# Layers two and three of a GraphSAGE kernel: 28 of 196 edge blocks as dense products of edge counts

## The reference

```
def _sage_layer(x, src, dst, inv_deg, W_self, W_neigh, b):
    agg = segment_sum(x[src], dst, num_segments=N_NODES)
    return x @ W_self + (agg * inv_deg[:, None]) @ W_neigh + b

h = relu(layernorm(x))
h = relu(_sage_layer(h, ..., W0_self, W0_neigh, b0))
h = relu(_sage_layer(h, ..., W1_self, W1_neigh, b1))
x = x + _sage_layer(h, ..., W2_self, W2_neigh, b2)
# second block: attention over the same edges (8 heads, edge scores s[src] + s[dst],
# softmax over the edges of each dst), output projection, batch norm, feed-forward, batch norm
x = x + L1_gnn(relu(layernorm(x)), ...)
```

## Time and profile before

| what | us |
|---|---|
| median of 3 runs | 6346.12 (6343.15 to 6388.92) |
| span of the profiled execution | 4316.7 |
| what lies between that span and the median | 2029.4 |
| layer one, first tile to first tile of layer two | 39.5 to 1036.3 |
| layer two | 1036.3 to 2025.4 |
| layer three, first tile to last tile | 2025.4 to 2985.6 |
| attention and feed-forward, to the end | about 1310 |

### The profile page before, as it was taken

How to read it: one execution, slowest core, us unless ns; L and a number is a source line. 1 busy time by engine, 2 the same in 40 slices (tenths; PEclk the granted TensorE clock), 3 DMA queues, 4 the chain that set the end, 5 groups by cost and what they waited for, 6 DMA issues and landing times. The chain is left out here.

```text
span 4316.7 us, 79500 instructions
## 1 busy us (share of the span) xinstructions
PE 3538.7 (82%) x15834; PEld 2475.2 (57%) x15925; DVE 2153.1 (50%) x6078; ACT 488.3 (11%) x1111; POOL 3031.3 (70%) x3154
## 2 busy tenths in 40 slices
PE   4898888888988888888888888888777777776798
PEld 3566565565655555655566665655655555555544
DVE  6434333333333333333455554555577777777733
ACT  4000000000000000000011101101011111111122
POOL 5777777777777777777777777776777777777200
PEclk9999999999999999999999999999788988897999
DMA  6444434434344344344444444445655555554411
GB/s 203 127 129 124 125 105 125 124 106 143 105 123 124 104 124 123 105 123 127 130 140 136 139 139 136 142 136 153 163 146 157 148 156 148 159 147 137 126 60 60
DMA packets 284796, 563.69 MB, mean 131 GB/s; under 512 B 104638, under 2 KB 176133, under 8 KB 279691
## 3 DMA queue, kind: packets, MB, share of 16 engines
q0 software_dynamic: 150528, 414.45, 33.7%
q10 hardware_dynamic: 70180, 89.46, 6.2%
q1 hardware_dynamic: 63974, 58.59, 4.4%
HBM read 487.19 MB, written 73.45 MB: 130 GB/s over the span
## 5 line engine op out<-in xcount | busy, mean ns | idle before, releaser
L763 POOL DMA_INDIRECT arena<-h_table,idx_v x2292 | 2183.6, 953 | 725.7 <-issue 692.9
L897 PE MATMUL banks<-arena 128*128 x5856 | 1465.2, 394 | 353.1 <-SPq L790 248.2
L897 PEld LDWEIGHTS banks<-arena 128*128 128x128 f32 x5856 | 1107.3, 194 | 678.2 <-issue 494.5
L842 DVE TENSOR_SCALAR arena<-iota_t,dst_e 128x128 f32<-128x128 f32 x2928 | 849.8, 306 | 797.2 <-PE banks L897 515.9
L1282 POOL DMA_INDIRECT arena<-vs_table,idx_v x764 | 766.6, 1003 | 232.8 <-issue 229.1
L900 PE MATMUL banks<-zeros 128*128 128x512 bf16 x2108 | 584.4, 385 | 4.6 <-issue 0.7
L1500 PE MATMUL banks<-arena 128*128 x1952 | 519.8, 417 | 53.1 <-DVE arena L1844 53.1
L1500 PEld LDWEIGHTS banks<-arena 128*128 128x128 f32 x1952 | 367.1, 199 | 193.1 <-issue 119.9
L952 DVE TENSOR_SCALAR small<-banks 128x1 f32<-128x1 f32 x147 | 23.3, 158 | 674.9 <-PE banks L901 674.9
L900 PEld LDWEIGHTS banks<-zeros 128*128 128x128 bf16 x2196 | 218.8, 100 | 202.2 <-issue 12.8
L1020 ACT ACTIVATE lhs<-banks 128x512 f32<-128x512 f32 x147 | 87.8, 597 | 2135.3 <-PE banks L911 2135.1
(11 more groups left out here) (265 smaller groups left out, 2505.3 us busy)
## 6 DMA issues: line engine op xcount, KB each, us to landing
arena<-h_table,idx_v POOLq DMA_INDIRECT x2292
arena<-dst_dram SPq DMA_DIRECT2D x14, 1792.0 KB
arena<-vs_table,idx_v POOLq DMA_INDIRECT x764
h_table<-arena ACTq DMA_DIRECT2D x11, 1024.0 KB, 7.5
h_early<-arena ACTq DMA_DIRECT2D x10, 1024.0 KB
vs_table<-arena ACTq DMA_DIRECT2D x49, 132.0 KB
x_dram<-arena ACTq DMA_DIRECT2D x49, 128.0 KB
hln_dram<-arena ACTq DMA_DIRECT2D x49, 128.0 KB
```

What stands on the lines that cost most here:

```text
L763: pool.indirect_dma_start(ring[:, s * BJ + j, 0:width], None, table, bass.IndirectOffsetOnAxis(idx_v[:, half, n * BJ + j:n * BJ + j + 1], ...
L842: dve.tensor_scalar(onehot[:, j, :], iota_t[:], dst_e[:, bass.ds(b * BJ + j, 1)], None, ALU.is_equal).then_inc(W["onehot_made"], 1)
L897: pe.matmul(agg[:, 0:D + 1], onehot[:, j, :], ring[:, (b % SLOTS) * BJ + j, 0:D + 1], start=False, stop=False).then_inc(W["onehot_used"], 1)
```

## The change

Of each seven blocks one may be picked whose `dst` values span at most COUNT_W = 41 nodes; 28 blocks are picked (NC), 168 stay in the list that is gathered (NB2). For a picked block the sum over its edges is written as a product: a matrix of counts (source node by `dst` offset, 6272 x 41) times the node rows.

1. **Picking.** In layer one, ahead of tile 5, `pick_tables_vector` and `pick_tables_tensor` choose the blocks and make new lists and spans: 62 VectorE instructions, each waiting for the one before, and six rounds with TensorE. `batch_tables_vector` moves from ahead of tile 8 to ahead of tile 3, `late_ends_vector` from ahead of tile 16 to ahead of tile 7. `batch_tables_scalar` (four DMAs) moves from behind layer one to behind tile 7 in layer one, and ScalarE waits there until they are done.
2. **Counting.** In tiles 8 to 23 of layer one, seven count blocks in every four tiles: VectorE makes two one-hots for each of the four columns (`low_hot`, 128 wide, and `count_hot`, 2016 wide, bf16), TensorE multiplies them into four banks (16 products of 128x512 bf16), ScalarE converts 2009 columns to int16, and each seventh time stores 3.6 MB to `counts_dram`.
3. **Folding.** For each of the 49 source tiles of the layer that is being made, ScalarE loads 128 x 1148 counts, converts them to fp32, and TensorE multiplies them with the tile's rows in `h_nodes`: CSLOTS = 9 fp32 products of 128x128 by 256, accumulated over all tiles in five banks. In layer one this is done in tiles 25 to 48, two in each; in layer two one in each tile. `folded_rows_vector` copies the 1148 sums into NV = 3 extra slots of the ring.
4. **The next layer** (`sums2`, `onehots2`) goes for each tile through its blocks of the list and then through its virtual blocks, with two sets of span and offset (`span_of`). Pairs of a layer: 168 + 48 and 3 + 48, 267 in all.
5. The products of zeros stay only in tiles 0 to 7 of layer one (four for each pair) and in layer three (one for each pair). The degree is kept from layer one (`inv_deg`), so `means` is one instruction in the layers behind it. In layer three `between` comes behind the blocks of the list.

The core of the diff:

```diff
+COUNT_W = 41
+TABLES_AT, PICK_AT, LATE_AT, COUNT_FROM = 3, 5, 7, 8
+COUNT_GROUP = 7
...
+        def count_block_vector(dve, i):
+            for j in range(BJ):
+                at = bass.ds(i * BJ + j, 1)
+                dve.wait_ge(counted, i * BJ + (COUNTED + j - 1))
+                dve.tensor_scalar(low_hot[j % 2], count_iota[:, 0:P], count_low[:, at], None, ALU.is_equal).then_inc(coded, 1)
+                dve.tensor_scalar(count_hot[j % 2], count_iota, count_code[:, at], None, ALU.is_equal).then_inc(coded, 1)
+
+        def count_block_tensor(pe, i):
+            pe.wait_ge(counts_taken, i + TAKEN)
+            for j in range(BJ):
+                pe.wait_ge(coded, i * (2 * BJ) + (CODED + 2 * j + 2))
+                for n in range(0, HOT_W, BE):
+                    to = min(n + BE, HOT_W)
+                    last = pe.matmul(banks[:, 4 + n // BE, 0:to - n], low_hot[j % 2], count_hot[j % 2][:, n:to], start=j == 0, stop=j == BJ - 1)
+                last.then_inc(counted, 1)
...
+        def counts_scalar(act, l, m, half, more=True):
+            s = m * 2 + half
+            act.wait_ge(counts_in[half], m * 16 + (COUNTS_IN[half] + 16 + 16 * l * ((NT + 1) // 2 - half)))
+            act.wait_ge(counts_used, s + (COUNTS_USED + l * NT - 1))
+            apart(act)
+            act.activation(counts[half], counts16[half], ACT.Copy).then_inc(counts_ready, 1)
+            if more:
+                act.wait_ge(counts_ready, s + (READY + l * NT + 1))
+                counts_load(act, s + 2, half)
...
+        def fold_tensor(pe, l, m, half):
+            s = m * 2 + half
+            pe.wait_ge(W["h_made"], since("h_made", l, s + 1))
+            pe.wait_ge(counts_ready, s + (READY + l * NT + 1))
+            apart(pe)
+            for c in range(CSLOTS):
+                n = min(P, CCOLS - c * P)
+                last = pe.matmul(banks[0:n, 3 + c // 2, c % 2 * D:c % 2 * D + D], counts[half][:, c * P:c * P + n], h_nodes[:, s, :],
+                                 start=False, stop=False)
+            last.then_inc(counts_used, 1)
...
+            def sums2(t):
+                wait(pe, W["mean_made"], since("mean_made", l, t))
+                pe.matmul(agg[:, 0:D], zeros[:, 0:P], zeros[:, 0:D], start=True, stop=False)
+                for h in range(2):
+                    b0, b1, off = span_of(pe, t, h)
+                    with pe.Fori(b0, b1 + 1) as b:
+                        pe.wait_ge(W["rows_ready"], since("rows_ready", l, b % NB2 + 1))
+                        slot = within(pe, b % SLOTS + b // NB2 * SLOTS, 0, SLOTS + NV - 1)
+                        for j in range(BJ):
+                            pe.wait_ge(W["onehot_made"], pair_at("onehot_made", l, b, off, j + 1))
+                            pe.matmul(agg[:, 0:D], onehot[:, j, :], ring[:, slot * BJ + j, 0:D],
+                                      start=False, stop=False).then_inc(W["onehot_used"], 1)
+                        if l == 2:
+                            pe.matmul(idle_ps, zeros[:, 0:P], zeros[:], start=True, stop=True)
...
             elif l == 1:
-                first_and_rest(pe, NT, step)
+                step(0)
+                pe.wait_ge(late_added, 2 * LATE)
+                fold_open(pe)
+                step(1)
+                fold_tensor(pe, 1, 0, 0)
+                with pe.Fori(1, NT // 2) as m:
+                    step(m * 2)
+                    fold_tensor(pe, 1, m - 1, 1)
+                    step(m * 2 + 1)
+                    fold_tensor(pe, 1, m, 0)
...
+            def two_with_counts(m):
+                step(m * 2)
+                counts_scalar(act, 1, m - 1, 1)
+                step(m * 2 + 1)
+                counts_scalar(act, 1, m, 0)
```

More of the change, by code:

```diff
@@ new lines, in fold_close, with folded_rows_vector @@
+        def fold_close(pe):
+            for i in range(3, 8):
+                last = pe.matmul(banks[:, i, :], zeros[:, 0:P], zeros[:], start=False, stop=True)
+            last.then_inc(folded, 1)
+        def folded_rows_vector(dve, l):
+            dve.wait_ge(folded, FOLDED + l)
+            if l == 1 and CSLOTS < NV * BJ:
+                dve.memset(ring[:, SLOTS * BJ + CSLOTS:(SLOTS + NV) * BJ, 0:D], 0.0).then_inc(rows_folded, 1)
+            dve.tensor_copy(ring[:, SLOTS * BJ:SLOTS * BJ + CSLOTS, 0:D],
+                            banks[:, 3:8, :].rearrange("p b n -> p (b n)")[:, 0:CSLOTS * D].rearrange("p (c d) -> p c d", d=D)
+                            ).then_inc(rows_folded, 1)
@@ L898, in sums @@
                                   start=False, stop=False).then_inc(W["onehot_used"], 1)
-                    for _ in range(4 if l < 2 else 1):
+                    for _ in range(idle):
                         pe.matmul(idle_ps, zeros[:, 0:P], zeros[:], start=True, stop=True)
@@ new lines, in sage_scalar @@
+                step(FOLD_FROM - 1)
+                act.wait_ge(counts_out, COUNTS_OUT + 16 * COUNT_GROUPS)
+                for half in range(2):
+                    counts_load(act, half, half)
+                with act.Fori(FOLD_FROM, 4 * GS) as t:
+                    with_counts(t)
+                store(3 * GS, GS)
+                with act.Fori(4 * GS, 5 * GS) as t:
+                    with_counts(t)
+                store(4 * GS, GS)
+                with act.Fori(5 * GS, NT - 2) as t:
+                    with_counts(t)
@@ new lines, in sage_scalar @@
+                store(NT - 1 - GS, GS - 1)
+                with_counts(NT - 2)
+                store(NT - 2)
+                counts_scalar(act, 0, NT // 2 - 1, 0)
+                counts_scalar(act, 0, NT // 2 - 1, 1, False)
+                counts_scalar(act, 0, NT // 2, 0, False)
+                step(NT - 1)
+                store(NT - 1)
+            elif l == 1:
+                act.wait_ge(counts_ready, READY + NT)
+                for half in range(2):
+                    counts_load(act, half, half)
+                step(0)
+                step(1)
+                counts_scalar(act, 1, 0, 0)
+                with act.Fori(1, GS // 2) as m:
+                    two_with_counts(m)
+                store(0, GS)
```

411 lines of the change are left out of this document (360 added, 51 removed).

## The result

The changed kernel takes 6952.3 us (median, 6945.0 to 6981.8), the kernel before 6347.2 beside it (6343.2 to 6405.0): a ratio of 1.093 [1.089, 1.098], slower by 605 us where the forecast was +357. The profiled execution took 6981.8 us with a span of 6980.0, so 1.8 us lie around a span.

A forecast was written before the change was run, and what follows sets the result against it. Gathers on GpSimd bound the kernel before, TensorE the changed layer two. Layers one, two and three, +212 + 109 + 36 = +357, made the span 4674 us; with 2029 carried over, 6703 us, slower by 5.6%, range 6060 to 6950.

The forecast's parts named there:

- Each layer goes at the pace of the gathers, 20.2 us a tile: Kernel before: GpSimd never waits and its gathers set each layer's pace, 989 / 49 = 20.2 us a tile.
- TensorE's own pace of 17.4 us: Layer one's first tiles, kernel before: TensorE alone needs 17.4 us a tile, a slack of 2.8 us.
- The 2029 us outside the span are shown by nothing; I carry them over: Whole kernel: timed 6346 us less profiled span 4317 us, added unchanged to the new span of 4674 us.
- Rival (a): Gathers: each costs 0.65 us more outside the profile, GpSimd stays the bound, 430 us go, 5916 us; chance 0.17.
- Layer one, +212: Layer one with tables, counting and folding: layer two starts at 1248 instead of 1036.3, +212 us (74 to 330).
- Tables +56: Layer one before tile 8: moved tables 13 us, picking 38, late ends 5, so tile 8 starts 56 us later.
- 16 x (23.3 - 20.2): Layer one, tiles 8 to 23: counting makes a tile 23.3 us, sixteen tiles 373 us.
- 23 x 3.1: Layer one, tiles 25 to 47: two folds and a late conversion make a tile 23.3 us, 23 tiles 534 us.
- Layer two, +109: Layer two: TensorE becomes the bound at 22.15 us a tile, 1098 us instead of 989, +109 (-50 to +195).
- layer three, +36: Layer three: a tile takes 20.75 us, first to last tile 996 us instead of 960, +36 (-19 to +91).
- The saved 284 us of GpSimd: Layers two and three: 112 gathers removed in each, 224 x 1.27 = 284 us of GpSimd.
- rival (d): TensorE's clock: falls with zeros gone and more waits, at 0.85 adding 290 us, near 6990 us; chance 0.04.
- Rival (b): TensorE keeps up, its tile under 17.4 us, the whole 284 us go: about 6137 us (6060 to 6283); chance 0.09.

The follow-up runs named there:

- run 4: Kernel before with one gather instead of four for each block in layers two and three, rows left incomplete: 5165.1 us, ratio 0.802.
- run 2: Kernel before without the four products of zeros behind each pair of layers one and two: 6651.6 us, ratio 1.035.
- run 5: Kernel before, GpSimd waiting for the last block's rows ahead of the next block's gathers, nothing left out: 6379.3 us, ratio 0.991.
- run 6: Changed kernel, GpSimd waiting for the last block's rows ahead of the next block's gathers, nothing left out: 6086.2 us, ratio 0.945.
- Run 7: Changed kernel with its dropped products of zeros put back in counting tiles, folding tiles and layer two: 7221.3 us, ratio 1.122.
- the copy: Kernel before, unchanged, profiled a second time: 6440.9 us, ratio 1.002, span 6396.4 us.
- 8 and 9: Kernel before and changed kernel, each with GpSimd waiting for the block before the last: 6365.2 us (1.002) and 6968.2 us (1.097).

## Why the prediction was right in direction and off in size

**The reading of the bound.** "Each layer goes at the pace of the gathers, 20.2 us a tile" was right for the profiled execution and wrong for the timed ones, where a tile takes 28.6 to 31.4 us. TensorE's own pace of 17.4 us was right: 17.6 with most gathers taken away (run 4).

**The step that failed** is "The 2029 us outside the span are shown by nothing; I carry them over". They are inside, and they are not a constant: part of them is time in which engines wait for late reports of TensorE, and the change lengthens these waits. Rival (a) put them on the gathers. For it spoke that they could not be launch: 1.8 us lie around a span here. The Trainium skill's "Runtime: NRT & Kernel Launch", in "The ~15µs preamble/postamble breakdown", has 9 to 15 us around a kernel; the runs agree with it only in that it is not 2029. The 30.7 us a tile of (a) came close to the 29.2 of layer two, but by luck: (a) made them 0.65 us a gather, which would be saved with it. A gather takes 1.25 us here too; its price is what stands still beside it.

**Layer one, +212, measured +569.** Tables +56 came to 74 up to tile 8. Counting was forecast 16 x (23.3 - 20.2) = 50 us over the tiles before and took 188, folding 23 x 3.1 = 71 over and took 291. My costs of the fold were about right in the timelines: 8.0 and 9.4 us for two (7.8 forecast), the conversion 1.85 us late (2.4). With pauses between gathers the same work costs 1640.2 - 1513.0 = 127 us, below my +212. What I missed is the mechanism by which the chain is paid in full on top of the gathers: with all four blocks of a tile free at once, GpSimd issues them in one run (16 for 4 and 12), during the run TensorE's reports are late and the other engines stand still, and then GpSimd waits itself. Of the 12 us that a counting or folding tile grew by, 5 are longer pauses (11 for 6) and 3 were forecast; the rest, at a lower clock and with less overlap, is not divided. That the runs are longer because the chain is, is argued: run 2, with less work in the chain, has runs of 16 as well.

**Layer two, +109, measured +69; layer three, +36, measured -47.** "TensorE is the bound, though the gathers got cheaper" is right in kind for layer two: GpSimd waits for slots, and TensorE's wait for rows is 0.3 us in 39 tiles. The sizes failed: 30.7 us a tile for 22.15, the conversion 4.8 us late for 2.4, and in layer three 30.8 for 20.75; paced it is 25.7 and 25.4. In layer three the direction was wrong too: the fewer gathers won over the longer loop. The saved 284 us of GpSimd appear once it sets the pace: from run 5 to run 6 layers two and three lose 202.9 and 228.9 us.

**The clock, rival (d).** It fell in layer one, 0.83 to 0.74, but follows the waiting: 0.86 in the same layer with the pauses. Run 7 raised it and lost time. The Trainium skill's "TensorE: Matmul & The Clock Gate", in "What's actually happening", has it that how busy the array was sets the clock. The rows bear that out in the main: 1.00 with TensorE busy 821 of 869 us (run 4), 0.74 with 1226 of 2078; but the copy's layer three, busy 1023 of 1509 us, has 0.74 and its layer one, 985 of 1509, has 0.83.

**Rival (b)**, 6137 with TensorE keeping up, is near run 6 (6086) in its number, and there GpSimd does set the pace, but at 25.7 us a tile and not at 17.4. The time came to 2 us above the upper end of my range, 6950, by a mechanism that none of my cases held; that it lies no further off is luck.

**Shown and open.** Shown: gathers issued without a pause are what the changed kernel loses by. A pause each four takes the remote waits away and more than the whole loss (run 6); a cap of eight without a pause does neither (8 and 9). What is late in a hold is TensorE's increments, in the semaphore records of the same traces; beside them some of SyncE's register instructions are slow (188 of 1865 take over 0.6 us in the changed kernel, 27 of 1862 in run 6, 2 of 2102 in run 5). Open: why a run of gathers delays these and not VectorE's increments, how long the pause must be, and why the execution of the earlier trace rows had gathers without a pause and yet no holds. No run told these apart.

## What to carry to other kernels

When the median stands far above the profiled span, don't carry the difference as a constant: take a second profile before costing anything. Look for engines that stand still until `remote`, compare the time of the increment that they waited for with the end of the instruction that raises it, and lay their idle time beside what GpSimd issues. If the standstills match runs of indirect gathers, break the runs with a wait that is not met at once (for the rows just asked for), and only then judge other changes: here one wait turned a loss of 9.3% into a gain of 5.5%. Judge the change against the kernel before with the same wait.

## What was not expected of the hardware

- Some 7.5 to 11 us into a run of gathers issued 1.25 us apart, the semaphore increments of TensorE come late, by up to 13.4 us for a tile's sum, and within 3 us of the run's end the engines go on. VectorE or ScalarE waits for the increment, and TensorE for them. VectorE's increments are in time (none of 3531 over 1 us late).
- A wait of 2.4 us behind each four gathers removed these pauses and cost the kernel before nothing (0.991); it took 12.5% off the changed one.
- Taking 20 products of zeros a tile from TensorE made the unpaced kernel 3.5% slower, and the paced one 0.9%.
